# Transposed one-hots kept in DRAM between two graph-attention layers, and ScalarE's fetched rows re-dealt: five a slot in the first layer, eight in the second

## The reference

```
xn = layernorm(x);  xp = xn + pos            # pos: a linear map of xn and of the node's degree
q, k, v = xp @ Wq, xp @ Wk, xp @ Wv
att = clip(sum(q[dst] * k[src]) / 4, -50, 50)            # for each edge and head
alpha = softmax of att over the edges with the same dst
x = x + segment_sum(v[src] * alpha, dst) @ Wo
x = x + gelu(layernorm(x) @ W1) @ W2
```

## Time and profile before

| what | value |
|---|---|
| three runs | 2118.71, 2124.51, 2126.39 us; median 2124.51 |
| profiled execution | 2124.16 us |
| its span, first to last instruction | 2122.4 us |
| POOL busy | 1523.3 us (72%), 1623 instructions |
| VectorE busy | 1710.6 us (81%) |
| TensorE busy, matmuls | 1372.7 us (65%) |
| ScalarE busy | 936.1 us (44%) |
| DMA | 290.07 MB, 137 GB/s in the mean |
| mean granted TensorE clock | 0.822 |

### The profile page before, as it was taken

The page is one execution under the profiler, slowest core; times in us unless marked ns, Lnnn a source line. Parts: engine busy times, 40 slices in busy tenths (PEclk is TensorE's granted clock), DMA queues, the critical chain, the costliest instruction groups (busy, mean ns, idle before and its releaser), DMA issues.

```text
span 2122.4 us, 44188 instructions
## 1 busy us (share of the span) xinstructions
PE 1372.7 (65%) x8158; PEld 1207.2 (57%) x8158; DVE 1710.6 (81%) x5189; ACT 936.1 (44%) x2180; POOL 1523.3 (72%) x1623
## 2 busy tenths in 40 slices
PE   4966666675766667666666656666665666656666
PEld 3655565565555656555555555555555555655555
DVE  8758999988888878888877778787787878788876
ACT  8333354443535354443544334334353535344344
POOL 6177777777777777777727777777777777777773
PEclk9978887878878797787988778877787978788778
DMA  3465455545444444444434444444444444444442
GB/s 90 125 175 146 148 153 153 153 135 150 140 145 130 146 139 141 135 140 145 133 100 137 139 140 138 132 140 143 139 134 139 142 140 129 143 140 136 134 141 62
DMA packets 134526, 290.07 MB, mean 137 GB/s; under 512 B 36564, under 2 KB 69648, under 8 KB 134256
## 3 DMA queue, kind: packets, MB, share of 16 engines
q0 software_dynamic: 77232, 206.41, 34.0%
q10 hardware_dynamic: 18016, 54.93, 8.2%
q1 hardware_dynamic: 39008, 25.91, 4.2%
HBM read 275.44 MB, written 8.38 MB: 134 GB/s over the span
## 4 chain that ended last, share of the span: by engine, by line
POOL 50%; issue 21%; DVE 9%; PE 7%; DMA 7%; ACT 3%; ACTq 1%; DVEq 1%; SPq 1%
POOL kvr L892 50%; DMA kvr<-kv_table,srcidx 6%; PE bank L1180 2%; DVE agg L1851 2%; PE bank L1193 2%; DVE kvr L1470 2%; ACT apart L1394 1%; ACTq L1429 1%; ACT onehotT L1398 1%; DVE msg L1838 1%; DVE onehot L1803 1%; PE bank L1137 1%; PE bank L992 0%; SPq L722 0%; DVE prod L1811 0%
## 5 line engine op out<-in xcount | busy, mean ns | idle before, releaser
L892 POOL DMA_INDIRECT kvr<-kv_table,srcidx x1567 | 1485.6, 948 | 535.4 <-issue 461.2
L1180 PE MATMUL bank<-q,onehotT 128*128 x3320 | 595.3, 335 | 700.2 <-DVE prod L1811 363.7
L1180 PEld LDWEIGHTS bank<-q,onehotT 128*128 128x128 f32 x3320 | 506.2, 233 | 810.0 <-issue 808.3
L1193 PE MATMUL bank<-msg,onehot 128*128 128x136 f32 x3320 | 601.3, 340 | 0.0
L1435 ACT ACTIVATE bank<-attc 128x32 f32<-128x32 f32 x404 | 81.2, 201 | 1102.9 <-DVE attc L1832 1059.6
L1193 PEld LDWEIGHTS bank<-msg,onehot 128*128 128x128 f32 x3320 | 562.4, 248 | 0.4
L1851 DVE TENSOR_TENSOR agg<-agg,bank 128x136 f32 x1624 | 468.9, 289 | 59.1 <-PE bank L1193 54.0
L1811 DVE TENSOR_TENSOR prod<-kvr,bank 128x512 f32<-128x512 f32 (+1 forms) x404 | 269.9, 668 | 283.9 <-DMA kvr<-kv_table,srcidx 244.5
L1394 ACT ACTIVATE apart<-relT,minus_p 128x512 bf16<-128x512 bf16 x416 | 293.8, 706 | 3.1 <-DMA relT<-rel_table 2.6
L1803 DVE TENSOR_TENSOR onehot<-bank,rel 128x512 f32<-128x512 f32 x416 | 282.5, 682 | 0.2
L1838 DVE TENSOR_TENSOR msg<-kvr,bank 128x512 f32<-128x512 f32 (+1 forms) x404 | 268.0, 663 | 11.4 <-ACT bank L1435 11.3
(11 more groups left out here) (224 smaller groups left out, 793.6 us busy)
## 6 DMA issues: line engine op xcount, KB each, us to landing
rowkv<-kv_table SPq DMA_DIRECT2D x4352, 1.0 KB
relT<-rel_table ACTq DMA_DIRECT2D x102, 512.0 KB
kvr<-kv_table,srcidx POOLq DMA_INDIRECT x1567
act_rowkv<-kv_table ACTq DMA_DIRECT2D x1408, 1.0 KB
loop_kv<-kv_table SPq DMA_DIRECT2D x25, 128.0 KB
kv_table<-qkv SPq DMA_DIRECT2D x25, 128.0 KB
kv_table<-onehot SPq DMA_DIRECT2D x8, 256.0 KB, 2.6
w<-weights SPq DMA_DIRECT2D x2, 840.0 KB, 7.3
```

Source lines behind the costliest of these rows:

```text
L892: pool.indirect_dma_start(kvr[:, n % RING, j, :], None, kv_table[l], bass.IndirectOffsetOnAxis(ap=srcidx[:, step:step + 1], axis=0)).then_ ...
L1180: mm = pe.matmul(bank[2][:, j * D:(j + 1) * D], onehotT[:, m % OHT, j, :], q[:, bass.ds(ranks[j + h], 1), :].rearrange("p a c -> p (a c)") ...
L1193: mm = pe.matmul(sum_ps(n, k), onehot[:, m % OH, j, :], msg[:, n % 2, j, :], start=(m, j) == of[0], stop=(m, j) == of[-1])
```

## The change

The transposed one-hots of the first layer are no longer made a second time for the second. The first layer's ScalarE stores each set, once made, to `hot_table` in DRAM (`save_hot`, 208 stores of 128 x 512 float32, 256 KB each); in the second layer it loads the sets from there (`load_hots`) at the place in its program where `edge_spread` stood, and makes none. A one-hot buffer in the first layer is written again only when its store has landed (`s_hot_saved`); TensorE in the second layer waits for the loads (`s_hot_loaded`) in place of `s_ohT`. The relT loads for the second layer go.

ScalarE's rows change with it: 5 a slot in the first layer, 8 in the second, and in the second layer more slots count as free: only those with a square root of layer norm 2 or with the feed-forward's activations are left out (`ACT_STD2`, `ACT_FF`, `ACT_FF + 1`). In numbers: the first layer has 118 free slots as before, 26 of them to a group, 4 groups in place of 5; the second has 165 in place of 151, 16 to a group, 10 groups in place of 6. POOL's gathers become 785 and 779.

```diff
-ACT_ROWS_A_SLOT, ACT_ROWS_A_LOAD, ACT_ROW_BUFS = 6, 8, 2
+ACT_ROWS_A_SLOT, ACT_ROWS_A_LOAD, ACT_ROW_BUFS = (5, 8), 8, 2
...
-    parts = {ACT_OUT, ACT_STD2, ACT_LN2, ACT_FF, ACT_FF + 1} | ({ACT_STD1, ACT_LN1, ACT_Q, ACT_LOOP} if l + 1 < L else set())
+    parts = {ACT_OUT, ACT_STD2, ACT_LN2, ACT_FF, ACT_FF + 1, ACT_STD1, ACT_LN1, ACT_Q, ACT_LOOP} if l + 1 < L else {ACT_STD2, ACT_FF, ACT_FF + 1}
...
+        hot_table = nc.dram_tensor("hot_table", [HOTS, P, G * P], F32, kind="Internal").ap()
...
                 ranks = read_ranks(ENG.PE, n)
-                pe.wait_ge(s_ohT, hots(n)[-1] + 1)
+                if n < GROUPS:
+                    pe.wait_ge(s_ohT, hots(n)[-1] + 1)
+                else:
+                    for m in hots(n):
+                        pe.wait_ge(s_hot_loaded[m % OHT], 16 * ((m - HOTS) // OHT + 1))
...
+            def save_hot(m):
+
+                act.wait_ge(s_ohT, m + 1)
+                act.dma_start(hot_table[m], onehotT[:, m % OHT, :, :].rearrange("p j e -> p (j e)")).then_inc(s_hot_saved[m % OHT], 16)
+
+            def load_hots(n):
+
+                for m in hots(n):
+                    if m == HOTS:
+                        save_hot(HOTS - 1)
+                    if m < HOTS + OHT:
+                        act.wait_ge(s_hot_saved[m % OHT], 16 * HOTS // OHT)
+                    act.wait_ge(s_qe, group_of(m - OHT) + 1)
+                    act.dma_start(onehotT[:, m % OHT, :, :].rearrange("p j e -> p (j e)"), hot_table[m - HOTS]).then_inc(s_hot_loaded[m % OHT], 16)
+
             def edge_spread(n):
 
+                if n >= GROUPS:
+                    load_hots(n)
+                    return
                 for h, m in enumerate(hots(n)):
+                    if m:
+                        save_hot(m - 1)
...
                     if m >= OHT:
                         act.wait_ge(s_qe, group_of(m - OHT) + 1)
+                        act.wait_ge(s_hot_saved[m % OHT], 16 * (m // OHT))
...
-                    if m % BODY == BODY - 1 and body < L * BODIES:
+                    if m % BODY == BODY - 1 and body < BODIES:
...
-                for p in range(row, min(row + ACT_ROWS_A_SLOT, P)):
+                for p in range(row, min(row + ACT_ROWS_A_SLOT[l], P)):
```

More of the change, by code:

```diff
@@ L169, in act_rows @@
         free = [s for s in range(6, 192) if act_is_free(l, s)]
-        each = -(-P // ACT_ROWS_A_SLOT)
+        each = -(-P // ACT_ROWS_A_SLOT[l])
         slots.append({})
@@ L178, in act_rows @@
             groups[l].append(g)
-            slots[l].update({s: (g, k * ACT_ROWS_A_SLOT) for k, s in enumerate(mine)})
+            slots[l].update({s: (g, k * ACT_ROWS_A_SLOT[l]) for k, s in enumerate(mine)})
     return slots, groups
@@ L569, in build @@
         s_ohT = sem("s_ohT")
+        s_hot_saved = [sem(f"s_hot_saved{u}") for u in range(OHT)]
+        s_hot_loaded = [sem(f"s_hot_loaded{u}") for u in range(OHT)]
         s_qe = sem("s_qe")
```

## The result

| | before | after |
|---|---|---|
| median of four runs | 2123.9 us | **2156.02 us** |
| lowest to highest | 2118.71 to 2126.39 | 2149.5 to 2162.43 |
| ratio, 95% interval | | 1.0146 [1.013, 1.0163] |
| profiled execution | 2124.16 us | 2162.43 us |
| its span | 2122.4 us | 2160.7 us |

The change makes the kernel slower by 32 us; forecast were 13 us, with 2119 to 2172 us for the range. The direction and the place were right, the size was not. The profiled execution of after is the longest of the four, 38.3 us over that of before; where those go is read first.

The account below looks back on a forecast made before the run. POOL's gathers bound the kernel before, at 4.83 us a group; a second-layer loop of 9.73 us for two groups would after. Median 2124.51 plus 8 (seams), 4 (other steps) and 1.25 (first layer) gave 2138 us, range 2119 to 2172.

Parts of the forecast that it names:

- POOL's gathers: Both layers' edge stages: 785 and 779 gathers at 1.253 us each, together -3.8 us if POOL stays the bound.
- The new wait and its loop: Second layer: the one-hot's load joins a loop over two groups, 6.48 us plus the load, 9.73 us against POOL's 9.66.
- X: Time from issue to landing of a 256 KB one-hot load in the second layer, taken as 3.25 us.
- The bounds, 2.6 and 3.7: Limits in us for the load's time, from a 256 KB store without gathers and a 416 KB load in 128 pieces.
- The rival that POOL stays the bound: Second layer: a load under 3.18 us fits the loop, only the gathers count, 2122 us; chance 40%.
- The one with X = 3.7: Second layer: load as slow as larger ones, loop 10.18 us, +56 us, 2180 us; 12% near it or beyond.
- TensorE takes the message sum of group n behind them ...: 1.08 or 1.96: Second-layer loop, query matmuls' end to VectorE's add: 1.08 us at full clock, 1.96 at half.
- The term for the load's issue: Second-layer loop: 0.26 us from the exponential to the load, the place of the first of two former activations.
- "ScalarE's rows hold up the exponentials": Second layer: late exponentials, taken as 0.1 us; at 0.4 us 29 us more, 2167 us; 4% of the own case.
- 195 x (4.87 - 4.85) = +4 us: Second layer's steps outside the seams: 4.87 us a group by the loop against 4.85 before, +4 us.
- The seams: Six groups at the second layer's start load two one-hots each; four within the loop, +8 us.
- The stores: First layer's one-hot stores: taken as nothing; a rival had gathers 2% longer, +20 us, 2140 us, chance 4%.

Follow-up runs that it names:

- the second run: The changed kernel with six rows a slot in both layers and the old free slots, loads still two groups ahead: 2144.48 us, ratio 1.0088.

## Why the prediction was right and wrong

- **POOL's gathers** (1564, 1.253 us each, bound of before): right. With the load or 0.6 us out of the loop, POOL is the bound again.
- **The new wait and its loop**: it is there, it sets the second layer's pace, and X is 3.24 us where 3.25 was taken. The bounds, 2.6 and 3.7, came from rows; that a value picked between them is right to 0.01 us is luck. The rival that POOL stays the bound falls: it needed X under 3.18 by the prediction's terms, and under 2.9 by the measured ones. The one with X = 3.7 falls too. Of the signs that were named, all are in the trace: 1564 gathers, the last product 30 us behind the last gather, TensorE waiting for the load in most groups, VectorE for the query matmul in place of the gathers.
- **The failed step** is "TensorE takes the message sum of group n behind them ...: 1.08 or 1.96", taken as 1.41 and measured as 1.82. It priced the passage from query matmuls to add from two places of a trace in which VectorE waited for TensorE. Two such loops share VectorE, one for even and one for odd groups, and VectorE has dense work besides; at 76% busy it is often not free when a query matmul ends (0.18 us a round behind the other loop, 0.14 behind the dense work). A sum of latencies over a loop that meets a busy engine is short by that engine's queue. 0.41 us x 97.5 rounds are 40 us. The term for the load's issue was too high (0.26, -0.03 in the trace) and gave 28 back, the exponentials took 9 and the small terms 8: some 28 in all. That a second error hid two thirds of the first is luck as well.
- **"ScalarE's rows hold up the exponentials"** was given 0.1 us and measured at 0.22 in all, 0.19 more than the bare 0.03; its price is the 11.5 us that the second run won back, exponentials, earlier landings and one gather of the first layer taken together. ScalarE does keep up in the mean, as forecast, but a loop that waits on it pays each time that it doesn't.
- **195 x (4.87 - 4.85) = +4 us** therefore became 29.8: a loop a hair over the bound was taken for a loop that costs a hair. An error of 0.28 us in 9.73, 3%, is 97.5 x 0.28 = 27 us here.
- **The seams**: +8 forecast, +5.8 measured.
- **The stores**: forecast at nothing, measured at 2.9 us. The even gathers behind one relT load could not show so little. Whether it is the gathers that get longer is not shown.

## What to carry to other kernels

A transfer that replaces computed data is to be placed by its latency and not by its bytes: issue it a whole stage earlier than the work that it replaces stood, or it enters the loop of the stages behind it. When a loop's sum lies within some per cent of the bound, add the queue at each shared engine in it before calling it hidden. And work that is given to an engine with free time (rows on ScalarE) costs what it delays on that engine, even where the engine keeps up in the mean.

## What the runs showed of the hardware

- A product on VectorE with both operands in SBUF lengthens POOL's indirect gathers: 948 to 967 ns in the mean with the order unchanged, 977 with it changed, the longest from 1.24 to 1.47 us; with the exponential in PSUM the same order leaves them at 946. Not every gather is lengthened: with the order unchanged 43 took over 1.1 us, and 41 of these began within 0.4 us of a message product's start and ended 0.82 us behind its end, as if held until it was done; in the changed kernel 51 began so and none was long. ScalarE's writing of the exponential is over by then, so it is VectorE's product. The Trainium skill, "SBUF — State Buffer", section "Who interferes with whom", has the rule: a VectorE instruction with two SBUF inputs contends with a GpSimd instruction that reads SBUF. These runs agree with it: the gather reads its row numbers from SBUF (`srcidx`). Which part of a gather is held up they do not tell.
- ScalarE's queue issues a load beside the activation that stands ahead of it: 1501.95 the exponential (0.20 us), 1501.96 the load's issue. The 0.26 us that lay between two activations is not there for a DMA.
- A load's landing depends on the row issues ahead of it in its queue: 3.14 us with six rows a slot, 3.24 with eight, of 256 KB each. A load completes in sixteen parts. In the changed kernel, of the 161 loads with all sixteen on record, the 55 that were issued within 0.6 us behind a row's issue take 3.41 us and the others 3.19, while fifteen parts are there after 2.95 us in both: one part is late.
- A DMA share of 0.71 with loads goes with gathers no longer than before (947.3 ns, 947.6 before).
